# Attention projections and the last MoE: one fp32 product in place of three rounded ones

## The reference

```python
x = x + attention(layernorm(x), Wq, Wk, Wv, Wo)      # causal, 16 heads of 8
x = x + recurrent_moe(layernorm(x), ...)             # 8 experts, top 2, two iterations
x = x + rwkv7(layernorm(x), ...)                     # linear attention scan
x = x + ffn(x, ...)                                  # the last MoE, below

bids = sigmoid(x @ conf_w.T + conf_b) * wealth       # 8 experts
top_bids, chosen = top_k(bids, 2); weight = softmax(top_bids)
# per expert e:  y = (silu(x @ gate_w[e].T) * (x @ up_w[e].T)) @ down_w[e].T
# gate_w, up_w: 512 x 128, down_w: 128 x 512 per expert
out = sum of weight * y over the two chosen experts
```

## Time and profile before

| | |
|---|---|
| median of 3 runs | 4220.74 us (4211.54 to 4229.47) |
| profiled execution, whole | 4258.15 us |
| its span | 4256.4 us |
| PE, PEld, DVE, ACT, POOL busy | 82%, 57%, 66%, 44%, 20% |
| chain of waits by engine | PE 54%, DVE 24%, ACT 11%, issue 7% |
| stage A, B, C, D, output in the span | to 875, 1853, 3818, 4208, 4256 us |

### The profile page before, as it was taken

The page is one execution under the profiler, slowest core; times in us unless marked ns, Lnnn a source line. Parts: engine busy times, 40 slices in busy tenths (PEclk is TensorE's granted clock), DMA queues, the critical chain, the costliest instruction groups (busy, mean ns, idle before and its releaser), DMA issues.

```text
span 4256.4 us, 69444 instructions
## 1 busy us (share of the span) xinstructions
PE 3484.6 (82%) x28042; PEld 2414.7 (57%) x28042; DVE 2805.6 (66%) x5367; ACT 1893.8 (44%) x3124; POOL 860.2 (20%) x907
## 2 busy tenths in 40 slices
PE   7999999975388989847888888888888888859995
PEld 4555555533255555525566566666666666648774
DVE  4666666633289889837777766666677676637775
ACT  3444444341377887724333333344333333216652
POOL 0003000002411221122221212222221221114553
PEclk7999999985699999969898898888888888859997
DMA  9997000001122122020000000000000000016666
GB/s 169 162 160 218 1 1 1 1 13 49 42 63 69 55 69 67 13 63 1 6 6 2 6 6 6 6 6 6 6 6 1 6 6 6 6 45 218 219 226 179
DMA packets 208113, 233.52 MB, mean 55 GB/s; under 512 B 12189, under 2 KB 182431, under 8 KB 201392
## 3 DMA queue, kind: packets, MB, share of 16 engines
q1 hardware_dynamic: 193712, 203.62, 20.0%
q0 software_dynamic: 14080, 25.45, 1.8%
HBM read 136.19 MB, written 96.48 MB: 55 GB/s over the span
## 4 chain that ended last, share of the span: by engine, by line
PE 54%; DVE 24%; ACT 11%; issue 7%; DMA 2%; SPq 1%; POOL 1%; another core or an unknown queue 0%; DVEq 0%; POOLq 0%; ACTq 0%
DVE t L2095 6%; PE ps L1501 5%; PE ps L1559 4%; PE ps L134 4%; PE ps L136 3%; PE ps L135 3%; PE ps L1591 3%; DVE t L477 2%; PE ps L1597 2%; PE ps L1600 2%; PE ps L852 2%; PE ps L333 2%; ACT t L979 2%; ACT t L977 2%; PE ps L859 1%
## 5 line engine op out<-in xcount | busy, mean ns | idle before, releaser
L2095 DVE COPY_PREDICATED t<-t,ps 128x512 f32<-128x512 uint32 x384 | 349.0, 909 | 102.9 <-PE ps L1559 96.0
L1501 PE MATMUL ps<-t 128*128 128x512 f32 x608 | 344.5, 679 | 33.1 <-DVE t L1961 15.0
L1871 ACT ACTIVATE t<-ps 128x512 f32<-128x512 f32 (+1 forms) x256 | 139.1, 544 | 511.5 <-PE ps L1600 401.9
L477 DVE TENSOR_REDUCE t<-ps 128x2 f32<-128x512 f32 (+1 forms) x512 | 260.7, 551 | 120.1 <-PE ps L292 119.9
L416 ACT ACTIVATE t<-ps 128x768 f32<-128x768 f32 x256 | 207.5, 811 | 252.5 <-PE ps L321 251.9
L134 PE MATMUL ps<-t 128*128 128x512 f32 (+1 forms) x660 | 279.7, 424 | 42.3 <-DVE t L503 25.8
L1591 PE MATMUL ps<-t 128*128 128x128 f32 x1280 | 242.7, 317 | 59.2 <-ACT t L1871 28.0
L1591 PEld LDWEIGHTS ps<-t 128*128 128x128 f32 x1280 | 199.6, 214 | 148.2 <-issue 85.4
L1559 PE MATMUL ps<-t 64*128 64x128 f32 x3072 | 239.8, 299 | 25.9 <-DVE t L2067 25.7
L136 PE MATMUL ps<-t 128*128 128x512 f32 (+1 forms) x660 | 258.8, 392 | 0.0
L135 PE MATMUL ps<-t 128*128 128x512 f32 (+1 forms) x660 | 258.6, 392 | 0.0
(11 more groups left out here) (424 smaller groups left out, 8744.8 us busy)
## 6 DMA issues: line engine op xcount, KB each, us to landing
t<-experts SPq DMA_DIRECT2D x39, 1536.0 KB
sorted<-t SPq DMA_DIRECT2D x4, 10855.0 KB, 145.9
t<-in_wP SPq DMA_DIRECT2D x92, 320.5 KB
experts<-t SPq DMA_DIRECT2D x8, 1536.0 KB, 6.1
t<-sorted SPq DMA_DIRECT2D x39, 260.0 KB
t<-answers SPq DMA_DIRECT2D x16, 512.0 KB, 6.7
t<-in_wE SPq DMA_DIRECT2D x8, 768.0 KB, 7.7
paired<-t SPq DMA_DIRECT2D x1, 6026.0 KB, 47.9
```

The costliest lines, as they stand in the source:

```text
L477: m = dve.e.tensor_reduce(nmf[:, z, blk * 16 + 4 * g + i0:blk * 16 + 4 * g + i0 + 2], ps[:, k:k + 2, a0:a1], AX.X, ALU.max, negate=True)
L1501: pe.e.matmul(ps[out, k, :], lhs, rhs, start=True, stop=True).then_inc(*e_pe(u, name))
L2095: dve.e.copy_predicated(out, msk.bitcast(U32), src).then_inc(*i_dve(k, "lev", li))
```

## The change

- `mm3` is gone. Each product it made is one fp32 matmul on unrounded operands.
- Stage A: no split of `wq`, `wk`, `wv`; `xn` has two buffers (one for each of two units) and is the matmuls' operand; ACT's copy and DVE's subtraction of step 2 are gone. The value projection is four fp32 matmuls.
- `prepare` keeps only the filling of the DRAM buffers; the splitting of expert weights and the tensor `experts` are gone.
- Stage D: the weights of a tile are loaded straight from `wE`, 128 x 1536 (768 KB for 1536 KB). Token tiles are copied once, by ACT. The product of silu and up is the operand of the down product; its ring `sg` has six buffers instead of four, and silu waits for the down product that read its buffer. POOL only scatters.

```diff
-def mm3(pe, out, a, b, start=True, stop=True):
-    pe.e.matmul(out, a[0], b[0], start=start, stop=False, skip_group_check=True)
-    pe.e.matmul(out, a[0], b[1], start=False, stop=False, skip_group_check=True)
-    return pe.e.matmul(out, a[1], b[0], start=False, stop=stop, skip_group_check=True)
...
-                pe.wait_ge(f_act, u, "hi")
-                pe.wait_ge(f_dve, u, "lo")
-                pe.wait_ge(w_lo, "wv")
+                pe.wait_ge(f_dve, u, "xn")
                 pe.wait_ge(*misc.free(n, u, g))
-                mm3(pe, ps[:, k, :], (wr[n][0][:, gs], wr[n][1][:, gs]),
-                    (xh[:, z, :], xl[:, z, :])).then_inc(*feat(u, n, g))
+                pe.e.matmul(ps[:, k, :], w[n][:, gs], xn[:, z, :], start=True, stop=True).then_inc(*feat(u, n, g))
...
-                    m = mm3(pe, ps[:, k, js], (xh[:, z, js], xl[:, z, js]), wr["wv"], start=(j == 0))
+                    m = pe.e.matmul(ps[:, k, js], xn[:, z, js], w["wv"], start=(j == 0), stop=True,
+                                    skip_group_check=True)
...
-                act.e.activation(xh[:, z, :], xn, ACT.Copy).then_inc(*f_act(u, "hi"))
...
-                dve.e.tensor_tensor(xl[:, z, :], xn, xh[:, z, :].bitcast(F32),
-                                    ALU.subtract).then_inc(*f_dve(u, "lo"))
+                dve.e.tensor_tensor(xn[:, z, :], xc[:, z, :], sq[:, z, :], ALU.mult).then_inc(*f_dve(u, "xn"))
...
-            pool.e.tensor_copy(out[:, z, 0:1536], raw[:, z, :]).then_inc(*hi(e))
-            pool.wait_ge(hi, e)
-            pool.e.tensor_tensor(out[:, z, 1536:3072], raw[:, z, :], out[:, z, 0:1536].bitcast(F32),
-                                 ALU.subtract).then_inc(*lo(e))
...
-            sp.e.dma_start(wts[:, i % 3, :].bitcast(F32), c.wS[bass.ds(own, 128), :]).then_inc(*w_in[i % 3](i))
+            sp.e.dma_start(wts[:, i % 3, :], c.aps["wE"][bass.ds(own, 128), :]).then_inc(*w_in[i % 3](i))
...
-            mm3(pe, ps[:, kg, :], parts(0), [a[:, z, :] for a in xr]).then_inc(*gate(i, h))
+            pe.e.matmul(ps[:, kg, :], gate_w, xr[:, z, :], start=True, stop=True).then_inc(*gate(i, h))
...
-            mm3(pe, ps[:, k, :], [wts[:, i % 3, s] for s in cs], [a[:, hq, :] for a in hhr],
-                start=(h == 0), stop=(h == 3)).then_inc(*downed(i, h))
+            pe.e.matmul(ps[:, k, :], wts[:, i % 3, 1024 + 128 * h:1152 + 128 * h], sg[:, (4 * i + h) % RING, :],
+                        start=(h == 0), stop=(h == 3)).then_inc(*downed(i, h))
...
-            if n >= 4:
-                h_low(act, *unit_at(n - 4))
-            act.e.activation(sg[:, n % 4, :], ps[:, kg, :], ACT.Silu).then_inc(*silu(i, h))
+            if n >= RING:
+                act.wait_ge(downed, *unit_at(n - RING))
+            act.e.activation(sg[:, n % RING, :], ps[:, kg, :], ACT.Silu).then_inc(*silu(i, h))
...
-            act.e.activation(hhr[0][:, n % 4, :], sg[:, n % 4, :], ACT.Copy).then_inc(*h_hi(i, h))
...
-                dve.e.tensor_tensor(hhr[1][:, n % 4, :], sg[:, n % 4, :], hhr[0][:, n % 4, :].bitcast(F32),
-                                    ALU.subtract).then_inc(*h_lo_dve(i, h))
```

More of the change, by code:

```diff
@@ L187, in stage_a @@
     identb, maskb = sb([128, 128], BF16), sb([128, 2, 256], BF16)
-    wr = {n: (sb(list(w[n].shape), F32R), sb(list(w[n].shape), F32R)) for n in ("wq", "wk", "wv")}
     xin = sb([128, 2, 8, 128])
@@ L357, in act @@
         act.wait_ge(c.loaded, "A")
-        for n in ("wq", "wk", "wv"):
-            act.e.activation(wr[n][0], w[n], ACT.Copy).then_inc(*w_hi(n))
         def load(g, _):
@@ L2582, in back @@
             m.then_inc(*y_pe(i))
-        do = dict(tile=tile, unit=unit, down=down, back=back, rest=lambda i, h: None)
+        do = dict(tile=tile, unit=unit, down=down, back=back)
         for step, i, h in steps_d():
@@ L2596, in tile @@
                 act.wait_ge(up, i - 2, 3)
-            act.e.activation(xr[0][:, i % 2, :], ps[:, k, :], ACT.Copy).then_inc(*x_hi(i))
+            act.e.activation(xr[:, i % 2, :], ps[:, k, :], ACT.Copy).then_inc(*x_act(i))
+            misc.give(("x", i), x_act, i)
         def unit(i, h):
@@ L2623, in down @@
                 acc.give(("y", i), y_act, i)
-        do = dict(tile=tile, unit=unit, down=down, rest=high)
+        do = dict(tile=tile, unit=unit, down=down)
         for step, i, h in steps_d():
@@ L2667, in back @@
             misc.give(("y", i), y_dve, i)
-        do = dict(tile=tile, unit=unit, back=back, rest=low)
+        do = dict(unit=unit, back=back)
         for step, i, h in steps_d():
@@ L2695, in back @@
                                           oob_is_err=False).then_inc(*sig)
-        do = dict(unit=unit, back=back)
         for step, i, h in steps_d():
-            if step in do:
-                do[step](i, h)
+            if step == "back":
+                back(i, h)
     return dict(pe=pe, act=act, dve=dve, pool=pool, sp=sp)
```

99 lines of the change are left out of this document (14 added, 85 removed).

## The result

The changed kernel takes 4264.92 us (median of 11 runs, 4249.34 to 4294.49), the kernel before in the same comparison 4229.0 (11 runs). The medians are 36 us apart. The ratio is 1.0094, 95% interval 1.0056 to 1.0131, which is 40 us of 4229: slower, clear of the noise, and about half of the 72 us of the prediction. The 11 runs of the changed kernel lie in two groups, five of 4249 to 4257 us and five of 4283 to 4294, with one between, so the 36 is not sharp: the interval is 24 to 55 us. The profiled execution took 4294.49 us, its span 4292.7.

What follows compares the result with a forecast made beforehand. TensorE was taken to bound stage D fully and stage A partly. D's +70 and A's +2 gave +72 us on the profiled 4258.15, 4330; carried to the timed median, 4293 us, 8-in-10 range 4262 to 4324.

Steps and rivals of the forecast that it cites:

- The product of D: Stage D: a native 512-column product takes 0.857 us instead of 0.699, over 468 products +74 us; a tile 11.2 us.
- Rival 1: Stage D: an fp32 product costs four rounded spacings of 0.233 us, +110 instead of +74, in all +108; chance 0.10.
- rival 4: Native instructions stream at the rounded spacing, a product 0.467 us: kernel faster, in all -151, 4070 us; chance 0.03.
- The rest of D: Stage D: PE's wait for POOL's remainder goes (-3.3 us), earlier first product (-2), start at the lower clock (+1).
- Rival 5: Stage D is paced by a release (silu, a bank), not streaming: 4221 less a few us; chance 0.03.
- Stage A at full clock: Stage A, each of 16 units: products +1.0, value projection -0.35, removed split operations -0.3: +0.35 us, +5 over all.
- the factor 0.8: Stage A: share of PE's added or saved time counted on the path, +1.26 us as +1.0; bounds 0.4 and 1.
- POOL's splitting: Stage A: removing POOL's splitting of the eight experts' weights saves 3 us, bounds -1 and -9.
- Stage A together: Stage A: +5 us from the units and -3 from POOL give +2; lower-clock stretches may move it +-15 either way.
- rival 2: Stage A gives more than it takes: -29 us there, all in all +41, 4262 us; chance 0.08.
- the signs named: Profile after: D's instructions 0.429 us apart, tile 11.2, PE busy at 1.00; A's units changed by less than 1 us.
- Rival 3: Stage A takes more: full product cost, no savings there, 15 us from the clock; all in all +104, 4325 us; chance 0.06.

Runs made afterwards that it cites:

- attention alone: Kernel before with only the changed stage A (native products, no splits there); POOL's splitting and stage D stay: 4209.17 against 4244.57 us, 0.9917.
- the two halves: Kernel before with only the changed stage A, 0.9917 (-35 us), and with only the changed stage D and weight preparation, 4312.05 us, 1.0163 (+67).

## Why the prediction was right and where it failed

1. **The product of D, +74.** Right. In D itself 0.430 us an instruction and 11.19 us a tile were measured, against 0.429 and 11.2; (268.50 - 224.00) / 24 x 39 = 72 us. Rival 1, four rounded spacings, and rival 4, a rate like the rounded one's, fell with the same rows.
2. **The rest of D, -3.3 - 2 + 1.** Measured D +65.6, so -7 for these. POOL's wait is gone (-3.3); the start is 2.2 us sooner. The cold start was forecast to cost 1 more and did not: the first four products took 4.97 us (by the loads at 3796.46 and 3801.43), before 4.86 (3827.57 and 3832.43), 0.1 more, where at full clock it would be 0.6. Rounded, all four ran at 1.2 GHz; native, the full clock was back after 3.5 us. Dead work on ACT and DVE changed D by 0.2 us: the cover was there, as said. Rival 5, a release as the pace, was wrong for before and after, but nearer than the prediction thought: taking a third of D's matmuls away gave no time at all.
3. **Stage A at full clock, +0.35 a unit.** Measured +0.11: the products +0.95 (forecast +1.0), the value projection -0.42 (-0.35), and step 2 what is left, 49.47 - 49.36 - 0.95 + 0.42 = -0.42 (-0.3), if the parts add. For the factor 0.8 on PE's work the runs have 0.95 / 1.26 = 0.75 and 0.42 / 0.45 = 0.93.
4. **POOL's splitting, -3.** Not measured by itself to this size. In the changed kernel its return cost nothing that the times show, and 6 us in one window; in the kernel with `norm` later it costs 18 us. The bounds of -1 and -9 were too narrow for what it can do.
5. **The step that failed is the clock in "Stage A together: +2", with "+-15" either way.** The prediction saw the mean clock of 0.94 and called it 50 us of loss at most, but took the change to be neutral to it and gave it no sign. Measured: attention alone -35 in time, and stage A -36 as the mean of four profiles each. Of these 36 us, 32 are what the steady windows are longer than at full clock (38 us on average with rounded products, 6.5 with native ones, POOL's part in it), 5 lie ahead of the first reciprocal (it starts at 100.1 to 101.1 us instead of 104.1 to 107.2), where the prediction had next to nothing and which no run takes apart, 1 lies at the end, and the 0.11 a unit takes 2 back. So the term that was put at nothing, with +-15, is worth some -30, an estimate. Its size could have been read from the trace of before: six of the 13 odd windows were at 23.6 us, and the others were 1.6 to 7.5 above it.

The time measured lies 3 us inside the lower end of the range, 4262 to 4324, but outside the +50 to +90 that had a chance of 0.70. That it fell into the range is luck as far as stage A goes: D was right, and the range reached down to rival 2, whose reasons did not come true. Of the signs named, D's all came (spacing, tile, PE at 1.00 and busy, DVE at 0.31, no wait for POOL, the product 2.2 us nearer, 437 us from first to last product). Stage A moved by over 15 us, though not at the same mean clock: 0.94 became 0.97.

Rival 2 gave 4262 us, nearly the time measured, but by another way: all of step 2's DVE time, -1.4 a unit, where the runs show -0.42, and 9 us for POOL. It is not confirmed by its number. Rival 3 has the sign of stage A wrong.

Shown by runs: the two halves add up within the noise; outside POOL's splitting the loss of clock needs the wait at L503 (moving `norm` took away both), and the same wait costs less or nothing when other matmuls stand in the window (native value, native products, or one product more). Not shown: why, after the same wait, a rounded odd window spends nothing, 3.5, 10 or 17 us at 1.2 GHz and a native one nothing or 3.5, and why equal code has 8 disturbed windows in one profile and none in another. A kernel with rounded products, `norm` later and the splitting in pieces was not tried; with 47.5 us a unit for 48.28 it should save a further 12 us, an estimate.

## What to carry to other kernels

When the mean clock of a stage is below 1, cut it into its repeating windows and list the length and clock of each before any edit is priced: here the loss was in a few windows, each behind one wait of PE, and it was worth more than all that the edit changed in that stage at full clock. An order by hand that puts a 1.75-us DVE operation ahead of something that PE wants is a thing to move early; here that gave 58 us for two changed numbers. Where PE is busy all the time (stage D), count instructions by their spacing; then ask which engine comes next, since a saving ends there.

## What the runs showed of the hardware

- A product of 512 columns costs 0.86 us on fp32 operands (two instructions) and 0.70 as three on fp32r; at 128 columns the native one is the cheaper, 0.22 us for 0.33 (three of 0.11).
- After a wait of 1.46 us TensorE ran on at 2.4 GHz in six odd windows of before, and at 1.2 GHz for some 3.5, 10 or 17 us, though busy, in the other seven; with native products (a wait of 1.3) for some 3.5 us or not at all. 0.70 us more of matmuls in the window, with the wait unchanged, made the kernel 28 us faster.
- Equal code differs by 16 to 20 us in stage A from profile to profile, so one profile each is too little to size an effect on the clock; in stage D, where the clock is 1.00 in all of the 24 tiles, the profiles of one form lie within 2.3 us.
- A DVE operation of 16 elements a partition took 3.43 us beside a POOL operation of 1536 columns; cut into 256 columns, POOL's work left DVE and the clock undisturbed.
